# Local attention of an AdaLN block in pairs of units: row tiles of 64 for the scores

## The reference, cut to what matters

```
q, k, v = split(layernorm(x) @ qkv_w, 3)            # 8 heads of 64
bq = q.reshape(b, h, nw, w, dh) * dh ** (-0.5)      # windows of w = 64
bk, bv = look_around(k), look_around(v)             # a window and both neighbours
sim = einsum('bhwid,bhwjd->bhwij', bq, bk)
sim = where(valid & (abs(t_q - t_k) <= w), sim, -max)
out = einsum('bhwij,bhwjd->bhwid', softmax(sim), bv)
light_out = out @ out_w
```

## Time and profile before

| | |
|---|---|
| median of three runs | 4289.97 us (4288.56 to 4294.81) |
| span of the profiled execution | 4290.7 us, the only time shown for that execution |
| TensorE busy | 3633.3 us (85%), 19,241 instructions |
| VectorE, ScalarE, GpSimd busy | 2510.6 (59%), 1932.9 (45%), 1495.8 us (35%) |
| mean granted TensorE clock | 0.914 |

### The profile page before, as it was taken

How to read it: one execution, slowest core, us unless ns; L and a number is a source line. 1 busy time by engine, 2 the same in 40 slices (tenths; PEclk the granted TensorE clock), 3 DMA queues, 4 the chain that set the end, 5 groups by cost and what they waited for, 6 DMA issues and landing times. The chain is left out here.

```text
span 4290.7 us, 59366 instructions
## 1 busy us (share of the span) xinstructions
PE 3633.3 (85%) x19241; PEld 2042.8 (48%) x19241; DVE 2510.6 (59%) x6732; ACT 1932.9 (45%) x4521; POOL 1495.8 (35%) x1807
## 2 busy tenths in 40 slices
PE   7378779987899879998799978998899988998787
PEld 2245444554446534465445544465444644455433
DVE  6754757366663667446573666536674575736652
ACT  5123435545254444554355542544445543545433
POOL 4133441254323451234422543234512444235311
PEclk8589899999899989997999988999899988999888
DMA  6210230002300231002300023002310023001120
GB/s 233 70 33 13 58 104 14 13 27 56 92 16 22 53 81 42 14 12 60 102 14 24 21 55 87 15 22 53 88 34 15 12 60 102 14 24 30 46 65 6
DMA packets 230687, 203.85 MB, mean 48 GB/s; under 512 B 11457, under 2 KB 212417, under 8 KB 230346
## 3 DMA queue, kind: packets, MB, share of 16 engines
q1 hardware_dynamic: 226338, 190.51, 15.9%
q0 software_dynamic: 3328, 8.39, 0.7%
q10 hardware_dynamic: 720, 1.15, 0.1%
HBM read 121.73 MB, written 77.69 MB: 46 GB/s over the span
## 5 line engine op out<-in xcount | busy, mean ns | idle before, releaser
L2330 ACT ACTIVATE arena<-pb 128x512 f32<-128x512 f32 (+3 forms) x1536 | 671.5, 491 | 342.6 <-PE pb L1565 337.5
L2410 POOL TENSOR_TENSOR arena<-arena,small 128x512 f32<-128x512 f32 x256 | 288.0, 1127 | 463.4 <-DVE small L1740 462.0
L2159 ACT ACTIVATE arena<-arena,small 128x256 f32<-128x256 f32 x512 | 256.0, 500 | 394.9 <-DVE small L1723 388.3
L2574 POOL TENSOR_SCALAR_AFFINE_SELECT arena<-arena 128x256 f32<-128x256 f32 x512 | 220.5, 433 | 544.7 <-ACT arena L2330 542.6
L1582 PE MATMUL pb<-arena,v 128*17 128x512 f32 (+3 forms) x3072 | 365.7, 506 | 32.9 <-POOL arena L2574 24.1
L2014 DVE TENSOR_REDUCE arena<-pb 128x1 f32<-128x512 f32 x512 | 329.8, 682 | 90.6 <-PE pb L1540 89.7
L1565 PE MATMUL pb<-arena 98*128 98x512 bf16 (+3 forms) x1152 | 355.3, 343 | 9.4 <-ACT arena L2330 5.7
L1723 DVE CUSTOM_DVE_ANT_0 arena<-pb,wmask 128x256 f32<-128x256 f32 x512 | 195.8, 419 | 218.5 <-PE pb L1282 218.3
L1282 PE MATMUL pb<-arena 128*128 128x256 f32 x1024 | 283.0, 401 | 5.4 <-issue 4.0
L1259 PE MATMUL pb<-hTf,wqkv 128*128 128x512 f32 (+1 forms) x640 | 245.8, 536 | 22.6 <-DVE hTf L1692 10.8
L1660 PE MATMUL pb<-xh,w1T 128*128 128x512 f32 x512 | 251.8, 640 | 9.7 <-DVE xh L1880 8.6
(11 more groups left out here) (354 smaller groups left out, 7588.8 us busy)
## 6 DMA issues: line engine op xcount, KB each, us to landing
arena<-split_q SPq DMA_DIRECT2D x64, 384.0 KB, 4.3
arena<-split_k SPq DMA_DIRECT2D x24, 768.0 KB, 7.1
split_q<-arena SPq DMA_DIRECT2D x64, 192.0 KB, 2.3
split_q<-arena SPq DMA_DIRECT2D x96, 128.0 KB, 2.0
split_k<-arena SPq DMA_DIRECT2D x64, 192.0 KB, 2.4
split_k<-arena SPq DMA_DIRECT2D x96, 128.0 KB, 2.1
arena<-split_k SPq DMA_DIRECT2D x24, 384.0 KB, 5.7
xn<-h_d SPq DMA_DIRECT2D x8, 1024.0 KB
```

The source lines that it names most:

```text
L2159: ins = s.activation(pm[n % 3][:, j], sm[n % 2][:, j], ACT.Exp, bias=nmx[:, 2 * sl + j:2 * sl + j + 1], scale=-1.0, accum_out=sml[:, 2 * s ...
L2330: s.activation(pp[pn % 4][:, h % 2, 0:w_], bank[n % 3][:, 0:w_], ACT.Exp).then_inc(a_exp1, 1)
L2410: g.tensor_tensor(pm[n % 3], pm[n % 3], rcl[:, 2 * sl:2 * sl + 2].unsqueeze(2).broadcast_to([P, 2, 2 * P]), ALU.mult).then_inc(p_norm0, 1)
L2574: g.affine_select(out=p2, in_=p2, pattern=[[0, 2], [1, P]], compare_op=ALU.is_ge, fill=0.0, base=0, channel_multiplier=-1).then_inc(p_tri, 1)
```

## The change

- `qt` holds q once, without zeros. Scores of head j contract over the 64 partitions of that head: both operands start at partition 64 j, so the products are row tiles of 64. Head 0 goes to bank 0 and head 1 to bank 1, two units to a bank. GpSimd's memsets of `qt` go, and q is taken out by one engine a tile.
- Units go in pairs of four steps. On TensorE: `turn(2m - 4)`; `scores(m)` for units 2m and 2m + 1 followed by `weigh(m - 3)` for two units; `turn(2m - 3)`; every second time a projection.
- Probabilities stay in one ring `ps` of six buffers: masking writes it, the exponential and the normalization work in place. `pt` has four buffers instead of two.
- One reciprocal serves two units.
- ScalarE copies the turned probabilities of unit 2m - 3 between the exponentials of 2m and 2m + 1; VectorE copies those of 2m - 4 ahead of its masking.

```diff
-    "begin": 1, "start": 1, ("light", 0): 17 + 2 * (UNITS + 6), ("light", 1): 12 + 2 * (UNITS + 6),
+    "begin": 1, "start": 1, ("light", 0): 17 + 4 * (PAIRS + 3), ("light", 1): 12 + 4 * (PAIRS + 3),
...
-        qt = view([H0 // 2, 2, NH])
+        qt = view([H0 // 2, NH])
...
-        sm = [view([2, 2 * P]) for _ in range(2)]
-        pm = [view([2, 2 * P]) for _ in range(3)]
-        pt = [view([4, P]) for _ in range(2)]
+        ps = [view([2, 2 * P]) for _ in range(6)]
+        pt = [view([4, P]) for _ in range(4)]
...
+                    def scores(m):
                         for j in range(2):
-                            mm = t.matmul(bank[bk][:, j * 2 * P:(j + 1) * 2 * P], qt[:, p_, j, i * P:(i + 1) * P], kt[:, p_, i * P:i * P + 2 * P],
-                                          start=True, stop=True)
+                            for w in left[j]:
+                                t.wait_ge(*w)
+                        for n in (2 * m, 2 * m + 1):
+                            i, p_ = divmod(n, H0 // 2)
+                            for j in range(2):
+                                mm = t.matmul(bank[j][:, (n % 2) * 2 * P:(n % 2 + 1) * 2 * P], qt[j * DH:(j + 1) * DH, p_, i * P:(i + 1) * P],
+                                              kt[j * DH:(j + 1) * DH, p_, i * P:i * P + 2 * P], start=True, stop=True)
                         mm.then_inc(t_s0, 1)
...
-                    for n in range(UNITS + 6):
-                        if n < UNITS:
-                            scores(n)
-                        if 0 <= n - 3 < UNITS:
-                            turn(n - 3)
-                        yield
-                        if 0 <= n - 4 < UNITS:
-                            weigh(n - 4)
-                        if n >= 8 and n % 4 == 0:
-                            project(n // 4 - 2)
-                        yield
+                    for m in range(PAIRS + 2):
+                        if m >= 2:
+                            turn(2 * m - 4)
+                        yield
+                        if m < PAIRS:
+                            scores(m)
+                        if m >= 3:
+                            weigh(m - 3)
+                        yield
+                        if m >= 2:
+                            turn(2 * m - 3)
+                        yield
+                        if m >= 5 and m % 2:
+                            project((m - 5) // 2)
+                        yield
+                    weigh(PAIRS - 1)
+                    yield
+                    project(TH - 1)
+                    yield
+                    yield
+                    yield
...
-                        if kind == "q":
-                            v.wait_ge(t_qkv, tn + n + 1)
-                            v.wait_ge(p_zero, 2 * (b + 1))
-                            v.tensor_scalar(qt[DH:P, m, 1, :], bank[bk][DH:P], DH ** -0.5, None, ALU.mult).then_inc(v_qkv, 1)
...
+                    for m in range(PAIRS + 2):
+                        yield
+                        if m < PAIRS:
+                            soften(2 * m)
+                        yield
+                        if m >= 2:
+                            turned(2 * m - 3)
+                        if m < PAIRS:
+                            soften(2 * m + 1)
+                        yield
+                        if m >= 4 and m % 2 == 0:
+                            take_out((m - 4) // 2)
+                        yield
...
-                    g.memset(qt[0:DH, :, 1], 0.0)
-                    g.memset(qt[DH:P, :, 0], 0.0).then_inc(p_zero, 1)
```

More of the change, by code:

```diff
@@ L200, in qkv_counts @@
     uses = qkv_uses(c)
-    return (sum(k == "q" or on_act(n) for n, (k, *_) in enumerate(uses)), sum(k == "q" or not on_act(n) for n, (k, *_) in enumerate(uses)))
+    return (sum(on_act(n) for n in range(len(uses))), sum(not on_act(n) for n in range(len(uses))))
 QKV_A, QKV_V = ([qkv_counts(c)[i] for c in range(2)] for i in range(2))
@@ L1262, in light @@
                         left[bk] = []
-                        if kind == "q" or on_act(n):
+                        if on_act(n):
                             an += 1
                             left[bk].append((a_qkv, an))
-                        if kind == "q" or not on_act(n):
+                        else:
                             vn += 1
@@ L1291, in turn @@
                         for j in range(4):
-                            mm = t.transpose(bank[2][:, j * P:(j + 1) * P], pm[n % 3][:, j // 2, (j % 2) * P:(j % 2 + 1) * P], ident[:, :])
+                            mm = t.transpose(bank[2][:, j * P:(j + 1) * P], ps[u % 6][:, j // 2, (j % 2) * P:(j % 2 + 1) * P], ident[:, :])
                         mm.then_inc(t_turn0, 1)
[L1294 to L1307, removed]
@@ new lines, in turn, with weigh @@
+                        left[2] = [(a_pt if n % 2 else v_pt, u // 2 + 1)]
+                    def weigh(m):
+                        for n in (2 * m, 2 * m + 1):
+                            i, p_ = divmod(n, H0 // 2)
+                            ob = 3 + i % 2
+                            if p_ == 0:
+                                for w in left[ob]:
+                                    t.wait_ge(*w)
+                            t.wait_ge(a_pt if n % 2 else v_pt, (UNITS * H + n) // 2 + 1)
+                            for blk in range(2):
+                                for j in range(2):
+                                    mm = t.matmul(bank[ob][j * DH:(j + 1) * DH, p_ * P:(p_ + 1) * P], vt[:, i + blk, 2 * p_ + j, :], pt[n % 4][:, 2 * j + blk],
+                                                  start=blk == 0, stop=blk == 1, skip_group_check=True)
+                            mm.then_inc(t_pv0, 1)
@@ L2143, in light @@
                                 s.wait_ge(p_halo, 2 * (b + 1))
-                            if kind == "k":
+                            if kind == "q":
+                                s.activation(qt[:, m], bank[bk], ACT.Copy, scale=DH ** -0.5).then_inc(a_qkv, 1)
+                            elif kind == "k":
                                 s.activation(kt[:, m, lo - c * NH:hi - c * NH], bank[bk][:, 0:hi - lo], ACT.Copy).then_inc(a_qkv, 1)
@@ L2178, in light @@
-                    for n in range(UNITS + 6):
-                        if n < UNITS:
-                            soften(n)
-                        if 0 <= n - 3 < UNITS:
-                            turned(n - 3)
+                        u = UNITS * H + n
+                        s.wait_ge(t_turn0, u + 1)
+                        if u >= 4:
+                            s.wait_ge(t_pv0, u - 3)
+                        s.activation(pt[n % 4].rearrange("p c q -> p (c q)"), bank[2], ACT.Copy).then_inc(a_pt, 1)
@@ L2183, in light, with take_out @@
+                    def take_out(i):
+                        s.wait_ge(t_pv0, UNITS * H + (i + 1) * (H0 // 2))
+                        if H or i:
+                            s.wait_ge(t_o0, TH * H + i)
+                        s.activation(onT.rearrange("p c q -> p (c q)"), bank[3 + i % 2], ACT.Copy).then_inc(a_on, 1)
+                    for m in range(PAIRS + 2):
                         yield
-                        if 0 <= n - 4 < UNITS:
-                            weigh(n - 4)
+                        if m < PAIRS:
+                            soften(2 * m)
@@ L2416, in project @@
                         g.tensor_tensor(x, x, xadd, ALU.add).then_inc(p_o0, 1)
-                    for n in range(UNITS + 6):
-                        if 0 <= n - 1 < UNITS:
-                            normalize(n - 1)
+                    for m in range(PAIRS + 2):
+                        if 1 <= m <= PAIRS:
+                            normalize(2 * m - 2)
                         yield
-                        if n >= 8 and n % 4 == 0:
-                            project(n // 4 - 2)
+                        if 1 <= m <= PAIRS:
+                            normalize(2 * m - 1)
                         yield
+                        yield
+                        if m >= 5 and m % 2:
+                            project((m - 5) // 2)
+                        yield
+                    yield
+                    project(TH - 1)
+                    yield
+                    yield
+                    yield
                 def hrows(b, _):
```

120 lines of the change are left out of this document (55 added, 65 removed).

## The result

The changed kernel takes 4301.53 us (median of 8 runs, 4296.19 to 4309.51) against 4291.81 for the kernel before (8 runs, the three of the table before among them): a ratio of 1.0028, with a 95% interval of 1.0018 to 1.0038. It is slower by about 0.3%, a small loss clear of the noise. The forecast was 88 us faster. The profiled execution has a span of 4300.5 us against 4290.7, and a mean granted clock of 0.902 against 0.914.

What follows compares the result with a forecast made beforehand. TensorE, busy 85% of the span, was taken as the bound; 48 us off seven c=0 halves, 36 off eight c=1 halves and 4 off the first half of all sum to 88, giving 4202 us, range 4162 to 4265.

Steps and rivals of the forecast that it cites:

- 1.72 us becomes 0.86 if they overlap wholly: Score products of a pair of units on TensorE: two heads' row tiles run two abreast, halving their time.
- Rival 2: Row tiles of the scores don't overlap: from 18 us off to 10 more, 4272 to 4300; chance 0.09.
- rival 3: Weight loads of the score row tiles exposed, 0.57 us more per pair: some 20 us off, 4270; chance 0.04.
- The changes of tile shape: TensorE switching between full, row and column tiles: 0.54 us per pair against 0.68, saving 0.14.
- The wait in the gaps of c=0: First halves, last four pairs: two without projection wait 0.98 us for ScalarE's copy, where they waited 0.39.
- Beside the MLP the other stage's matmuls fill it: First four pairs of c=0 halves: MLP matmuls cover the new wait; 6.8 us saved per half, 48 over seven.
- a nanosecond taken off TensorE should be a nanosecond of the end: Seven c=0 halves, TensorE busy 482.9 of 514 us: saved work shortens the kernel equally, unless a wait replaces it.
- I take the middle, 4.5 us: Eight c=1 halves, beside norm, MLP and rotary chains: saving between 0.2 and 8 us each; 36 us in all.
- VectorE's copies now stand ahead of the masking, so the 1.3 us should go: Transposes in a c=1 half: their 1.3 us wait for VectorE's copy of turned probabilities disappears.
- The clock was named as a risk: Sign against the prediction: granted clock of c=1 halves, 0.93, falls further as TensorE's work thins out.
- Rival 4: Slower: ScalarE's copy behind exponentials makes c=1 pairs wait 2.3 us, 83 us lost less 52 from c=0: 4321; chance 0.05.
- The first half of all: The half beside the first global attention: saving between 0 and 8 us, taken as 4.

Runs made afterwards that it cites:

- e2_old_half: The kernel before with one of the two score products of each unit left out, in the old order: 4244.43 us.
- e7_tstw: The changed kernel reordered: even unit's transposes, scores, odd unit's transposes, values, with ScalarE copying ahead of both exponentials: 4249.24 us.
- e9_half_masks: e7_tstw with one of VectorE's two maskings of each unit left out: 4228.06 us.
- e10_half_exps: e7_tstw with one of ScalarE's two exponentials of each unit left out: 4222.38 us.
- e11_half_norm: e7_tstw with GpSimd normalizing only the first head of each unit: 4213.95 us.
- e5_early_project: The changed kernel with each projection four steps earlier and ScalarE's copy of the weighed values one step earlier: 4332.77 us.
- e6_copy_first: The changed kernel with ScalarE's copy of the odd unit's transposes ahead of both exponentials of the pair: 4279.25 us.
- e1_order_full: The changed kernel's order with score products on the full tile of 128 rows instead of row tiles: 4351.42 us.
- e14_tstw_by_half: e7_tstw with both exponentials of a pair in one ScalarE step in the c=0 halves only: 4237.98 us.

## Why the prediction was wrong, point by point

- **"1.72 us becomes 0.86 if they overlap wholly": right.** 1.06 us for eight score instructions with the change of shape. Rival 2 (no overlap) and rival 3 (exposed loads) are out. The rule on weight loads that the prediction takes from the Trainium skill's "TensorE: Matmul & The Clock Gate", part 3, that they overlap running matmuls only where the row group differs (the same part excepts loads into a background buffer), does not hold here. By the prediction's estimate, three exposed loads of 0.19 us would have put the block at 1.6 us.
- **The changes of tile shape: right**, 3.05 us of TensorE a pair against 3.16.
- **The wait in the gaps of c=0: right in size, too small in number.** 0.98 forecast for one wait, 1.10 measured in the same terms. One c=0 half (820 to 895 us) waited 3.3 us for ScalarE's copy in four waits, where 1.96 in two were counted, and with it 1.7 us for the chains' normalized tile, 1.4 us in the MLP's first layer and 1.3 us for VectorE's copy, which were counted at nothing. TensorE's idle time grew by 4.9 us a c=0 half, not by the 1.2 of the sum.
- **"Beside the MLP the other stage's matmuls fill it" and "a nanosecond taken off TensorE should be a nanosecond of the end": failed, and 46 us of the miss with it.** The step gave 6.8 us a half in c=0; 0.3 came. Even in the old order, at the full clock, 6.9 us of work are worth 4.8 (e2_old_half): in a stretch that is 94% busy the waits for the copies grow as the work goes. Of the 6.5 us a half that are missing, about 3.7 are idle time beyond the forecast's and 2.9 are busy time that did not go, 2.0 of them against the one half that kept the full clock. e7_tstw, with the same row tiles, has about 5 us back, idle time and clock together.
- **"I take the middle, 4.5 us" in c=1: failed, and it is the other 46 us.** The middle between two ends has no reason behind it when the stage isn't TensorE's. The halves got 1.2 us longer: idle time grew by 5.8 us where the sum had 3.5, and busy time fell by 4.6 where it had 8.0. In the old order 6.9 us of work are worth 1.2, and e9_half_masks, e10_half_exps and e11_half_norm show that no single engine is the bound; the earlier trace rows showed 85% and 70% busy. The clock takes a part that the forecast put at nothing, 2 to 4 us a half by the estimate above.
- **"VectorE's copies now stand ahead of the masking, so the 1.3 us should go": wrong.** 24.9 us became 27.3. The transposes that wait for VectorE's copy have scores and values ahead of them in the new order; why the wait did not shrink was not tested. It grew in e2_old_half (35.8) as well, so lighter TensorE work is enough to lengthen it.
- **Not foreseen:** the projections come six steps later (all but the last), and TensorE waits 38.4 us for the chains' normalized tile against 18.8. e5_early_project moved the projections and didn't recover it, and why it grew stays open. It is not what separates the slow order from the fast one, for it is 42.0 us in e6_copy_first and 41.3 in e7_tstw, which are both faster. The transposes wait 14.6 us for GpSimd (1.8 before); one reciprocal for two units may be the reason, and was not tried alone. The clock was named as a risk and had no price. In c=0 it explains 2.0 of the 2.9 us by which busy time fell short of the 8.0 us of work.
- **Rival 4 was the right kind of case with the wrong accounting.** It wanted 1.8 us of waiting in each c=1 pair against c=0 halves that gain 52 us. What happened is a gain of nothing in c=0 and a small loss in c=1. The sum by halves: 7 x (-0.3) + 8 x 1.2 = +7.5. The first half of all ends 1.0 us earlier, where the sum had 4. The rest, some 3 us of the 9.8, is in the q, k, v stretches and between the halves, and was not followed up.

## What to carry to other kernels

Before crediting work saved on the busiest engine, ask what it meets when it arrives earlier: an engine at 94% may have the other engines' results just ahead of it, and one at 85% in a stage full of handshakes need not be the bound. Ask also what its clock does when it idles more: here a part of the saved work went into running the rest at the lower clock. When two producers into one buffer follow each other with nothing between them, the copy out of that buffer stands bare, and its place in the copying engine's order (behind or ahead of work that needs new input) can be worth more than the faster arithmetic. Here one copy's place on ScalarE was worth 55 us between its best and its worst, the whole new order cost more than the row tiles gave, and the same row tiles in an order with both copies covered made the kernel 1.0% faster.

## What the runs showed of the hardware

Two float32 row tiles of 64 x 128, writing different banks, run fully abreast: eight instructions of 256 columns take 1.06 us to the start of the column tiles behind them, where eight full ones take 1.82 in e1_order_full (2888.04 to 2889.86). Their weight loads, 182 to 187 ns each, are hidden in that time. In this kernel the tiles take a bank each. TensorE's granted clock followed how thin its work was: in the c=1 halves 0.91 to 0.98 before and 0.86 to 0.88 in the change, in the c=0 halves 1.00 and 0.95 to 1.00. With the same steps and nearly the same waits, a c=1 half granted 0.88 was 4.0 us longer than one granted 0.95 (e14_tstw_by_half and e7_tstw).
